# Local attention in steps of two windows: row tiles for the scores, column tiles for the weighted sums

## The chip, the cores and the metric

The kernel runs on one core of one Trainium2 chip. The metric is the device time of one execution in microseconds (us). A core has a matrix engine (TensorE, PE in the profile, with its weight loads as PEld), a vector engine (VectorE, DVE), an activation engine (ScalarE, ACT), a general engine (GpSimd, POOL) and a queue engine that issues transfers (SyncE, SP). Each works through its own list of instructions in order; semaphores join the lists. On chip, data lie in SBUF (128 partitions) and in PSUM, which TensorE writes, in banks of 512 float32 columns per partition.

## The reference, cut to what matters

The program is four blocks of attention and feed-forward on `x` (8 x 256 x 256), with a layer norm before each. The stage that the change touches is the third attention. With 16 heads of 16 elements, windows of 64 rows, and each window attending to itself and to the window before it:

```python
qb = q.reshape(b, h, nb, w, d) * d ** -0.5           # w = 64, d = 16, 4 windows in a batch
kw, vw = look_around(kb), look_around(vb)            # the window before, then this one: 128 keys
sim = jnp.einsum('bhnwd,bhnjd->bhnwj', qb, kw)
sim = jnp.where(mask[None, None], sim, -jnp.finfo(sim.dtype).max)
attn = jax.nn.softmax(sim, axis=-1)
out = jnp.einsum('bhnwj,bhnjd->bhnwd', attn, vw)
...
return x @ W_out.T + b_out
x = x + jnp.tanh(g_xattn[2]) * _L2_xattn_ref(_layernorm(x, axis=-1), ctx_1024, ctx_1024, L2_xattn_W_out, L2_xattn_b_out)
```

## The kernel before

`build` runs nine stages one after the other, with a barrier between them. All but `stage_local_attention` (L1558 to L1912) stay as they are.

**A unit** is one window of one batch: 4 units in a batch, 8 batches, 32 units. The 16 heads are taken as 8 pairs, since a pair's 2 x 64 query rows fill 128 rows. The 256 features lie in two halves (`kt`) of 128 partitions with four pairs in each. GpSimd writes `la_qd` (L1896): for each half, four stationary matrices of 128 x 128, in which only the 32 partitions of the pair hold queries and all others are zero. So each score product runs over all 128 partitions, although 32 of them count.

**One unit on TensorE**, in the names of the trace:
- `front`, L1702 and L1704, twice: a product with the identity puts the mask into a bank of `la_scores` (512 columns), and four products `la_qd` x `la_kT` are added to it. Four banks, so that two units have room.
- `turn`, L1718: eight transposes of `la_e` into two banks `la_turned`.
- `back`, L1730: eight products `la_eT` (stationary, 128 x 128) x `la_vw` (33 columns: the values of a pair of heads and a column of ones for the sum of the weights) into `la_av`.

Each float32 product shows as two pairs of records, weight load and matmul; a transpose as one.

**The other engines.** VectorE takes the maximum of a bank (L1812) and subtracts it while it copies the bank to `la_e` in SBUF (L1817). ScalarE takes the exponent in SBUF (L1778), one instruction for 512 columns, and copies `la_turned` to `la_eT` (L1787). VectorE takes the reciprocal of the 8 sums (L1829) and multiplies (L1833).

**Once a batch.** `prep`: TensorE transposes queries and context (L1685, L1691) through the one bank of `la_misc`, and ScalarE copies them out (L1765, L1770). `final`: TensorE transposes the attention's output (L1739), ScalarE copies it (L1791), TensorE multiplies by `la_woT` (L1746), VectorE adds to `x_res` (L200), and the layer norm follows.

**The order** is written by hand in `batches`: per unit `turn(n)`, `front(n+1)`, `back(n)`, so TensorE has the scores of the next unit to do while the weights of this one are copied. Batches 1 to 6 are a loop over two batches. At the start, GpSimd adds the bias to all 16 tiles of `x_res` (L1914) before its first `la_qd`.

## Time and profile before

| | us |
|---|---|
| median of 3 runs | 2733.89 (2731.76 to 2738.29) |
| the profiled execution | 2743.94 |
| its span | 2742.2 |
| of this, local attention, first instruction to last | 1634.35 to 1877.36 |
| first score product of the stage | 1657.4 |

The profile is one execution, recorded by the hardware. Its span runs from the first to the last instruction; 1.7 us of the execution lie outside. Start times are counted from the span's start. A group of consecutive instructions of one kind stands in one row, with its first start and the time to its last end. Matmuls overlap in the engine, so their starts lie closer together than one takes. The granted clock is a share of TensorE's full speed (2.4 GHz); 0.5 is 1.2 GHz.

### The profile page before, as it was taken

The numbers are of one execution on the slowest core, as the hardware profiler recorded it, in microseconds if no ns is written. First come the engines' busy times: TensorE is split into PE (matmuls) and PEld (weight loads), VectorE is DVE, ScalarE is ACT, GpSimd is POOL, SyncE is SP. The second block draws the span as 40 slices with busy tenths as digits, with TensorE's granted clock in tenths as the row PEclk, the third lists the DMA queues.
The fourth block names the chain that finished last, engine by engine and source line by source line (L and its number), as shares of the span: only waits on it lengthen the run. The fifth ranks groups of instructions, "written<-read, shape, count | busy, mean of one in ns | idle before, by whom it ended". The sixth has DMA issues, their size and how long they took to land. (4 is left out here: it accounts for less than half of the span.)

```text
span 2742.2 us, 39081 instructions
## 1 busy us (share of the span) xinstructions
PE 2031.4 (74%) x12230; PEld 1715.1 (63%) x12265; DVE 1472.1 (54%) x4679; ACT 785.6 (29%) x2012; POOL 512.1 (19%) x670
## 2 busy tenths in 40 slices
PE   4178699999999759999999807885910667777445
PEld 3155477777777759999999807883510655566323
DVE  5789755555555421111111155676577538988856
ACT  2111133333333211111111103442463423333155
POOL 3567610000000040000000064340024320000110
PEclk9589899999999779999999958996965785567569
DMA  2100010000000260032132131211000030111100
GB/s 92 32 1 0 14 73 4 8 8 8 8 8 0 89 236 25 23 117 71 69 117 71 47 97 28 43 21 35 0 0 0 0 109 26 36 28 35 26 21 31
DMA packets 133827, 113.56 MB, mean 41 GB/s; under 512 B 60384, under 2 KB 118760, under 8 KB 133736
## 3 DMA queue, kind: packets, MB, share of 16 engines
q1 hardware_dynamic: 120280, 94.67, 11.3%
q10 hardware_dynamic: 10384, 9.45, 1.0%
q0 software_dynamic: 3072, 8.39, 0.9%
q8 instruction: 38, 0.62, 0.1%
q14 instruction: 53, 0.43, 0.0%
HBM read 78.00 MB, written 24.05 MB: 37 GB/s over the span
## 5 line engine op out<-in xcount | busy, mean ns | idle before, releaser
L1481 DVE TENSOR_TENSOR me_h<-me_sg,me_ps_u 128x512 f32<-128x512 f32 x106 | 72.9, 688 | 346.9 <-PE me_ps_u L1412 346.9
L1412 PE MATMUL me_ps_g<-me_xT,me_w 128*128 128x128 f32 x1696 | 208.5, 276 | 12.9 <-DMA me_w<-in_L_ffn_w_s 12.9
L1412 PEld LDWEIGHTS me_ps_g<-me_xT,me_w 128*128 128x128 f32 x1696 | 203.2, 193 | 16.4 <-DMA me_w<-in_L_ffn_w_s 13.3
L1412 PE MATMUL me_ps_u<-me_xT,me_w 128*128 128x128 f32 x1696 | 207.5, 276 | 0.0
L1421 PE MATMUL me_ps_y<-me_w,me_h 128*128 128x256 f32 x848 | 200.6, 379 | 0.0
L1412 PEld LDWEIGHTS me_ps_u<-me_xT,me_w 128*128 128x128 f32 x1696 | 198.8, 193 | 0.0
L989 ACT ACTIVATE ca_e<-ca_main,ca_neg_max 128x256 f32<-128x256 f32 x256 | 119.1, 470 | 211.0 <-DVE ca_neg_max L1037 211.0
L1421 PEld LDWEIGHTS me_ps_y<-me_w,me_h 128*128 128x128 f32 x848 | 152.9, 190 | 16.4
L1461 ACT ACTIVATE me_sg<-me_ps_g 128x512 f32<-128x512 f32 x106 | 63.3, 597 | 337.6 <-PE me_ps_g L1412 337.6
L902 PE MATMUL ca_main<-ca_kT,ca_qT 128*128 128x256 f32 x512 | 135.9, 394 | 4.4 <-DVE carrier L79 3.6
L925 PE MATMUL ca_av<-ca_v,ca_eT 128*128 128x64 f32 x1024 | 131.1, 272 | 8.5 <-DVE ca_eT L1033 8.5
L1530 POOL DMA_INDIRECT mc_picked<-moe_y_list,moe_slot x32 | 31.3, 978 | 564.4 <-SPq L1507 554.6
L925 PEld LDWEIGHTS ca_av<-ca_v,ca_eT 128*128 128x128 f32 x1024 | 125.3, 193 | 12.6 <-DVE ca_eT L1033 7.8
L2279 PE MATMUL id_ps_h<-ident,id_h 128*128 128x128 f32 x96 | 14.5, 292 | 145.2 <-DVE id_h L2302 145.2
L180 POOL TENSOR_TENSOR ca_ln_rstd<-ca_ln_mean_var,eps 128x1 f32<-128x1 f32 x16 | 3.1, 192 | 560.1 <-DVE ca_ln_mean_var L174 560.1
L2636 PE MATMUL ss_acc<-sc_gm,ss_zT 32*128 32x128 f32 (+2 forms) x368 | 83.5, 379 | 30.3 <-ACT ss_zT L2517 30.3
L2508 ACT ACTIVATE sc_y_all<-ss_v 128x16 f32<-128x16 f32 x256 | 60.4, 236 | 158.3 <-DVE ss_v L2570 156.0
L1486 DVE COPY me_y<-me_ps_y 128x256 f32<-128x256 f32 x53 | 22.5, 424 | 154.7 <-PE me_ps_y L1421 154.7
L2279 PEld LDWEIGHTS id_ps_h<-ident,id_h 128*128 128x128 f32 x96 | 12.3, 151 | 147.6 <-DVE id_h L2302 145.1
L2636 PEld LDWEIGHTS ss_acc<-sc_gm,ss_zT 32*128 32x128 f32 x368 | 67.8, 266 | 54.7 <-ACT ss_zT L2517 54.7
L1026 DVE TENSOR_TENSOR ca_main<-ca_main,ca_mask_add 128x512 f32<-128x512 f32 x128 | 88.8, 694 | 22.6 <-PE ca_main L902 21.3
L902 PEld LDWEIGHTS ca_main<-ca_kT,ca_qT 128*128 128x128 f32 x512 | 90.1, 192 | 16.0 <-DVE carrier L79 6.5
(420 smaller groups left out, 4755.9 us busy)
## 6 DMA issues: line engine op xcount, KB each, us to landing
me_w<-in_L_ffn_w_e SPq DMA_DIRECT2D x24, 1024.0 KB, 8.7
ss_gb<-scan_g_band SPq DMA_DIRECT2D x15, 512.0 KB, 3.9
me_x_tile<-moe_x_list SPq DMA_DIRECT2D x54, 128.0 KB
moe_y_list<-me_y ACTq DMA_DIRECT2D x53, 128.0 KB
moe_x_list<-mr_zeros SPq DMA_DIRECT2D x1, 5248.0 KB, 23.4
la_vw<-in_ctx SPq DMA_DIRECT2D x24, 128.0 KB, 3.4
x_res<-in_x SPq DMA_DIRECT2D x4, 512.0 KB, 8.0
fa_q<-x_norm SPq DMA_DIRECT2D x8, 256.0 KB, 2.4
```

Of the source, the lines that this page charges most:

```text
L902: last = nc.tensor.matmul(ps[:, it * S:(it + 1) * S], qT[:, s // 2, s % 2, it * P:(it + 1) * P], kT[:, s // 2, :], start=True, stop=True)
L925: last = nc.tensor.matmul(ps_av[g % 2][:, o:o + DH], eT[:, h % 2, jt, it * P:(it + 1) * P], v[:, jt, h * DH:(h + 1) * DH], start=(jt == 0) ...
L989: last = nc.scalar.activation(e[:, h % NE, it, :], ps[:, it * S:(it + 1) * S], ACT.Exp, bias=neg_max[:, h % 4, it:it + 1], accum_out=sums[ ...
L1026: nc.vector.tensor_tensor(both, both, mask_add[:, bass.ds(b, 1), :].broadcast_to([P, 2, S]), ALU.add).then_inc(masked, 1)
L1412: last = nc.tensor.matmul(ps[:, j * P:(j + 1) * P], w13[:, buf, w, kt, f:f + P], xT[:, kt, :], start=(kt == 0), stop=(kt == KD - 1))
L1421: last = nc.tensor.matmul(ps_y[:, 0:D], h[:, c, j, :], w2[:, buf, f, :], start=(f == 0), stop=(f == FT - 1))
L1461: nc.scalar.activation(sg[:, c, :], ps_g[c][:, :], ACT.Silu).then_inc(silu_done, 1)
L1481: nc.vector.tensor_tensor(h[:, c, :, :].rearrange("p j n -> p (j n)"), sg[:, c, :], ps_u[c][:, :], ALU.mult).then_inc(h_ready[c], 1)
L1530: nc.gpsimd.indirect_dma_start(out=picked[:, t % BUFS, j, :], out_offset=None, in_=y_list, in_offset=bass.IndirectOffsetOnAxis(ap=slot[:, ...
L2279: last = nc.tensor.transpose(ps_h[c][:, j * P:(j + 1) * P], h[:, par, f * P:(f + 1) * P], core.ident[:, :])
L2508: nc.scalar.activation(y_all[:, :, :, t], by_batch(v[:, :, t]), ACT.Sigmoid).then_inc(y_ready, 1)
L2636: last = nc.tensor.matmul(acc[n % 2][:, h, 0:P].rearrange("p (b t) -> p b t", b=B)[:, :, c0:TB], zT[rows, k, h, :], gm[rows, pair(n, k), : ...
```

## The change

The step is now two windows (`NU` = 2), 16 steps in all, and the loop is written out in full. The stationary operand of a score product is 32 partitions high, one pair of heads, so that four pairs lie in four row tiles of the array, each writing a bank of its own. In the weighted sums the operands are swapped: the values of a pair (32 columns: 16 of one head and 16 zeros, or the reverse, from `la_vz`) are stationary, `la_eT` (64 columns) moves, and four pairs write four column tiles of 32 partitions. The sums of the weights come from the same products with a matrix of ones (`la_ones`), on all 32 partitions, so the reciprocal now has 256 columns. The output comes out transposed, so that L1739 and L1791 go. The maximum is taken negated, the subtraction goes, and ScalarE takes it as the bias of the exponent, straight from PSUM, one instruction for each 128 columns.

```diff
-        def batches(eng, walks, prep, turn, front, back, final, finish):
...
-                    turn(b, par, nb)
-                    if nb < UNITS - 1:
-                        front(b, par, nb + 1)
-                    elif has_next:
-                        front(b + 1, 1 - par, 0)
-                    back(b, par, nb)
...
+        def walk(prep, score, turn, weigh, final, finish):
+
+            prep(0)
+            for n in range(STEPS + 1):
+                b, u = divmod(n, NU)
+                if n >= 1:
+                    for r in range(RT - 1):
+                        turn(n - 1, r)
+                if n < STEPS:
+                    score(n)
+                if n >= 1:
+                    turn(n - 1, RT - 1)
+                if u == 0 and b + 1 < B:
+                    prep(b + 1)
+                if n >= 1:
+                    weigh(n - 1)
+                if u == 1 and b >= 1:
+                    final(b - 1)
+                if u == 0 and b >= 2:
+                    finish(b - 2)
...
+            sp.wait_ge(const, 3)
+            load(0)
...
+            def score(n):
+                b, u = divmod(n, NU)
+                pe.wait_ge(q_ready, n + 1)
...
+                banks = [ws.fill() for _ in range(RT)]
...
+                for ps, _, _ in banks:
+                    nc.tensor.matmul(ps[:, :], ident16[:, :], masks[:, int(u > 0), :, :], start=True, stop=False)
+                for j in range(4):
+                    nb, kt = divmod(j, KD)
+                    lo = W * (NU * u + nb)
+                    for r, (ps, filled, _) in enumerate(banks):
+                        rows = slice(R * r, R * (r + 1))
+                        last = nc.tensor.matmul(ps[:, j * P:(j + 1) * P], qd[rows, n % 2, kt, nb, :],
+                                                kT[rows, b % 2, kt, lo:lo + P], start=False, stop=(j == 3))
...
+            def turn(n, r):
+                ws.when_read(score_bank[n, r])
+                ps, filled, turned_bank[n, r] = wt.fill()
...
+            def weigh(n):
+                b, u = divmod(n, NU)
+                pe.wait_ge(vz_ready, b + 1)
+                for r in range(RT):
+                    wt.when_read(turned_bank[n, r])
                 ps, filled, _ = wa.fill()
...
+                for j in range(4):
+                    nb, kt = divmod(j, KD)
+                    for what in range(2):
+                        o = (4 * what + j) * W
+                        for h in range(2):
+                            for r in range(RT):
+                                lhs = (ones[:, h, :, :] if what else
+                                       vz[:, b % 2, NU * u + nb, RT * kt + r, 2 * h:2 * h + 2, :])
+                                last = nc.tensor.matmul(ps[R * r:R * (r + 1), o:o + W],
+                                                        lhs.rearrange("p a d -> p (a d)"),
+                                                        eT[:, n % 2, r, j, h * W:(h + 1) * W],
+                                                        start=(h == 0), stop=(h == 1))
...
+            def final(b):
+                wa.when_all_read()
...
+            def exponent(n, r):
+                act.wait_ge(max_done, RT * n + r + 1)
+                for j in range(4):
+                    last = nc.scalar.activation(e[:, n % 2, r, j, :], scores.ps[r][:, j * P:(j + 1) * P], ACT.Exp,
+                                                bias=mx[:, n % 2, r, j:j + 1])
+                    if j == 3:
+                        last.then_inc(scores.empty[r], 1)
+
+            def turn(n, r):
+                if r == 0:
+                    exponent(n, 0)
+                if r < RT - 1:
+                    exponent(n, r + 1)
+                ps, empty = wt.drain()
...
+                half = NU * KD * W
+                nc.vector.reciprocal(rsum[:, :], ps[:, half:2 * half]).then_inc(recip, 1)
...
+            nc.gpsimd.memset(vz[:, :, :, :, :, :], 0.0).then_inc(const, 1)
+            nc.gpsimd.memset(vn[0:W, :, 0, :], 0.0).then_inc(const, 1)
...
-            with pool.Fori(0, TILES) as t:
-                nc.gpsimd.tensor_tensor(core.x[:, t, :], core.x[:, t, :], bias[:, :], ALU.add).then_inc(bias_added, 1)
```

TensorE, in the first batch, two units before the change. `la_scores0` to `3` and `la_turned0` and `1` are the banks:

```order
L1718 MATMUL la_turned0<-ident,la_e 128x128 x4
L1718 MATMUL la_turned1<-ident,la_e 128x128 x4
L1702 MATMUL la_scores0<-la_masks,la_ident16 128x512
L1704 MATMUL la_scores0<-la_kT,la_qd 128x128 x4
L1702 MATMUL la_scores1<-la_masks,la_ident16 128x512
L1704 MATMUL la_scores1<-la_kT,la_qd 128x128 x4
L1730 MATMUL la_av0<-la_vw,la_eT 128x33 x8
```

The same place after it, one step of two units: the end of one step's transposes, the scores of the next (the last line comes four times in turn over the banks), and the weighted sums (this pair of lines comes four times):

```order
L1708 MATMUL la_turned0<-ident,la_e 128x128 x4
L1693 MATMUL la_scores0<-la_masks,la_ident16 128x512
L1693 MATMUL la_scores1<-la_masks,la_ident16 128x512
L1693 MATMUL la_scores2<-la_masks,la_ident16 128x512
L1693 MATMUL la_scores3<-la_masks,la_ident16 128x512
L1699 MATMUL la_scores0<-la_kT,la_qd 128x128
L1699 MATMUL la_scores1<-la_kT,la_qd 128x128
L1699 MATMUL la_scores2<-la_kT,la_qd 128x128
L1699 MATMUL la_scores3<-la_kT,la_qd 128x128
...
L1708 MATMUL la_turned1<-ident,la_e 128x128 x4
L1725 MATMUL la_av0<-la_eT,la_vz 32x64 x8
L1725 MATMUL la_av0<-la_eT,la_ones 32x64 x8
```

Before, the scores of one unit use two banks of four. Now a step uses all four, and its first instruction needs all four read.

ScalarE at the same place, before, for two units:

```order
L1778 ACTIVATE la_e<-la_e 128x512 x2
L1787 ACTIVATE la_eT<-la_turned0 128x512
L1787 ACTIVATE la_eT<-la_turned1 128x512
L1778 ACTIVATE la_e<-la_e 128x512 x2
L1787 ACTIVATE la_eT<-la_turned0 128x512
L1787 ACTIVATE la_eT<-la_turned1 128x512
```

And after, for one step:

```order
L1763 ACTIVATE la_e<-la_scores0,la_mx 128x128 x4
L1763 ACTIVATE la_e<-la_scores1,la_mx 128x128 x4
L1776 ACTIVATE la_eT<-la_turned0 128x512
L1763 ACTIVATE la_e<-la_scores2,la_mx 128x128 x4
L1776 ACTIVATE la_eT<-la_turned1 128x512
L1763 ACTIVATE la_e<-la_scores3,la_mx 128x128 x4
L1776 ACTIVATE la_eT<-la_turned0 128x512
L1776 ACTIVATE la_eT<-la_turned1 128x512
```

The exponents of banks 2 and 3 now stand behind copies that wait for TensorE's transposes of the same step.

## Rows read from the trace of the kernel before

**Rows 1.** Busy time by stretch: PE, PEld, DVE, ACT, POOL; granted clock; DMA share, GB/s
```profile
1634.30:1657.40 23.10, 3.32 (x12) 2.15 (x12) 0.35 (x1) 3.08 (x4) 18.03 (x30) 0.50 0.54 102
1657.40:1877.40 220.00, 190.87 (x1470) 178.34 (x1496) 141.55 (x384) 85.86 (x150) 75.83 (x94) 0.97 0.13 27
```

**Rows 2.** Waits of 1657 to 1877.5: waiter, waited for: total us, times, longest
```profile
PE la_turned L1718 <- ACT la_e L1778: 9.7, 18, 1.4
...
PE la_misc L1746 <- ACT la_aoT L1791: 7.2, 8, 0.9
```

**Rows 3.** Timeline, PE, once a batch: start us, us, engine, line, operation, count [idle]
```profile
1725.64 1.97 PE L1746 MATMUL la_misc<-la_woT,la_aoT 128*128 128x256 f32 x8 [0.92 <-ACT la_aoT L1791]
...
1751.71 1.97 PE L1746 MATMUL la_misc<-la_woT,la_aoT 128*128 128x256 f32 x8 [0.92 <-ACT la_aoT L1791]
```

**Rows 4.** Timeline, PE, parts of units at full clock
```profile
1771.43 1.04 PE L1718 MATMUL la_turned<-ident,la_e 128*128 128x128 f32 x8
...
1773.41 0.38 PE L1702 MATMUL la_scores<-la_masks,la_ident 128*128 128x512 bf16 x1
1773.63 1.05 PE L1704 MATMUL la_scores<-la_kT,la_qd 128*128 128x128 f32 x8
1774.52 0.31 PE L1730 MATMUL la_av<-la_vw,la_eT 128*128 128x33 f32 x2
```

**Rows 5.** Groups by line, PE: count | busy us, mean ns | idle before
```profile
L1730 PE MATMUL la_av<-la_vw,la_eT 128*128 128x33 f32 x512 | 60.0, 272 | 0.0
```

**Rows 6.** Timeline, later stages: row tiles (32*128), full array, column tiles (128*32), bfloat16
```profile
2400.21 0.66 PE L2636 MATMUL ss_acc<-sc_gm,ss_zT 32*128 32x128 f32 x4
2400.80 0.60 PE L2627 MATMUL ss_acc<-sc_gm,ss_zT 128*128 128x128 f32 x3
...
2402.32 0.14 PEld L2653 LDWEIGHTS ss_ps_z<-ident,ss_z 128*32 128x32 f32 x2 [0.56 <-DVE ss_z L2606]
...
2660.12 0.62 PE L2970 MATMUL bt_ps_h<-bf_ident,bt_hi 128*128 128x128 bf16 x8 [1.17 <-DVE bt_hi L2933]
```

**Rows 7.** Timeline and groups, ACT: exponents, small activations, the copy of `la_turned`
```profile
821.01 0.47 ACT L989 ACTIVATE ca_e<-ca_main,ca_neg_max 128x256 f32<-128x256 f32 x1 [1.33 <-DVE ca_neg_max L1037]
821.38 0.19 ACT L989 ACTIVATION_READ_ACCUMULATOR ca_e<-ca_main,ca_neg_max 128x1 f32 x1
...
2399.57 0.22 ACT L2508 ACTIVATE sc_y_all<-ss_v 128x16 f32<-128x16 f32 x1
2399.69 0.22 ACT L2512 ACTIVATE ss_az<-ss_v 128x16 f32<-128x16 f32 x1
...
L1221 ACT ACTIVATE mr_ex<-mr_shifted 128x128 f32<-128x128 f32 x1 | 0.3, 309 | 3.6 <-DVE mr_shifted L1248 3.6
...
1781.82 1.09 ACT L1787 ACTIVATE la_eT<-la_turned 128x512 f32<-128x512 f32 x2 [4.18 <-PE la_turned L1718]
```

**Rows 8.** Groups, DVE: reciprocals of 8 and of 96 columns, a product of 256
```profile
L1829 DVE RECIPROCAL la_rsum<-la_av 128x8 f32<-128x8 f32 x32 | 6.6, 206 | 2.5 <-PE la_av L1730 1.6
...
L525 DVE RECIPROCAL f4p_q_rscale<-f4p_q_scale 128x96 f32<-128x96 f32 x2 | 1.5, 752 | 0.1
...
L1047 DVE TENSOR_TENSOR ca_ao<-ca_av,ca_rsums 128x256 f32<-128x256 f32 x64 | 24.2, 419 | 1.1
```

**Rows 9.** Timeline, the stage's start, and GpSimd's largest memset (group)
```profile
L1071 POOL MEMSET ca_qT<- 128x4096 f32 x1 | 3.5, 3512 | 1.3 <-POOLq L93 1.3
...
1643.60 0.35 DVE L1801 TENSOR_SCALAR la_bias<-la_bias,tanh_g 128x256 f32<-128x256 f32 x1 [12.23 <-DMA la_bias<-in_L_xattn_b_out]
...
1648.51 0.60 ACT L1770 ACTIVATE la_kT<-la_misc 128x512 f32<-128x512 f32 x1 [1.21 <-PE la_misc L1691]
1655.18 4.29 POOL L1896 TENSOR_TENSOR la_qd<-la_xT,la_own 128x512 f32<-128x512 f32 x4
```

**Rows 10.** Timeline, the stage's end: the last output product and the last layer norm
```profile
1870.32 3.38 PE L1746 MATMUL la_misc<-la_woT,la_aoT 128*128 128x256 f32 x8 [0.78 <-ACT la_aoT L1791]
...
1876.95 0.41 DVE L194 TENSOR_SCALAR x_norm<-x_res,la_ln_mean_var,la_ln_rstd 128x256 f32<-128x256 f32 x1 [0.44 <-POOL la_ln_rstd L183]
```

More of the change, by code:

```diff
@@ L18 @@
 I32 = mybir.dt.int32
+I16 = mybir.dt.int16
+U16 = mybir.dt.uint16
 U8 = mybir.dt.uint8
@@ L1631, in nothing @@
         def nothing(*_):
             pass
[L1634 to L1640 removed]
         @block.sync
         def _(sp):
[L1644 to L1656 removed]
+            wm = Walk(misc, sp)
@@ L1669, in _ @@
         @block.tensor
         def _(pe):
-            ws, wt, wa, wm = walks(pe)
-            pe.wait_ge(small_in, 32)
-            ps, filled, use = wm.fill()
-            for kt in range(KD):
-                for r in range(2):
-                    last = nc.tensor.transpose(ps[:, (kt * 2 + r) * P:(kt * 2 + r + 1) * P],
-                                               wo[:, r, kt * P:(kt + 1) * P], core.ident[:, :])
-            last.then_inc(filled, 1)
-            def prep(b, par):
-                pe.wait_ge(xs_in[par], 32 * (b // 2 + 1))
+            ws, wt, wa, wm = (Walk(banks, pe) for banks in (scores, turned, av, misc))
@@ L1745, in final @@
                     for kt in range(KD):
-                        last = nc.tensor.matmul(ps[:, h * D:(h + 1) * D], aoT[:, kt, h * P:(h + 1) * P], woT[:, kt, :],
-                                                start=(kt == 0), stop=(kt == KD - 1))
+                        last = nc.tensor.matmul(ps[:, h * D:(h + 1) * D], aoT[:, b % 2, kt, h * P:(h + 1) * P],
+                                                woT[:, kt, :], start=(kt == 0), stop=(kt == KD - 1))
                 last.then_inc(filled, 1)
-            pe.wait_ge(const2, 2)
-            batches(pe, list(zip((ws, wt, wa, wm), PER)), prep, turn, front, back, final, nothing)
+            weights()
+            walk(prep, score, turn, weigh, final, nothing)
         @block.scalar
         def _(act):
-            ws, wt, wa, wm = walks(act)
+            wt, wm = Walk(turned, act), Walk(misc, act)
             nc.scalar.preload_act_table(ACT.Exp)
@@ L1794, in _ @@
-            batches(act, list(zip((ws, wt, wa, wm), PER)), prep, turn, front, nothing, final, nothing)
+            def exponent(n, r):
+                act.wait_ge(max_done, RT * n + r + 1)
+                for j in range(4):
+                    last = nc.scalar.activation(e[:, n % 2, r, j, :], scores.ps[r][:, j * P:(j + 1) * P], ACT.Exp,
+                                                bias=mx[:, n % 2, r, j:j + 1])
+                    if j == 3:
+                        last.then_inc(scores.empty[r], 1)
@@ new lines, in turn @@
+            def turn(n, r):
[4 more added lines that the diff above has]
+                ps, empty = wt.drain()
+                if r == 0 and n >= 2:
+                    act.wait_ge(av.filled[0], n - 1)
+                nc.scalar.activation(eT[:, n % 2, r, :, :].rearrange("p j q -> p (j q)"), ps[:, :], ACT.Copy
+                                     ).then_inc(empty, 1)
+            walk(prep, nothing, turn, nothing, lambda b: wm.skip(1), nothing)
@@ L1796, in _ @@
         @block.vector
         def _(dve):
-            ws, wt, wa, wm = walks(dve)
+            ws, wa, wm = (Walk(banks, dve) for banks in (scores, av, misc))
             wm.skip(1)
@@ L1830, in back @@
                 dve.wait_ge(recip, n + 1)
-                to = W * (nb % 2)
-                for h in range(2):
-                    last = nc.vector.tensor_tensor(
-                        ao[to:to + W, par, nb // 2, :].rearrange("p (g c) -> p g c", g=PAIRS)[:, :, h * DH:(h + 1) * DH],
-                        sums[h * W:(h + 1) * W, :, h * DH:(h + 1) * DH],
-                        rsum[h * W:(h + 1) * W, nb % 2, :].unsqueeze(2).broadcast_to([W, PAIRS, DH]), ALU.mult)
-                last.then_inc(empty, 1)
@@ L1847, in final, with finish @@
                 core.vector_inc(empty)
-            def finish(b, par):
+            def finish(b):
                 for h in range(2):
                     norm.vector_apply(dve, 2 * b + h, h)
-            batches(dve, list(zip((ws, wt, wa, wm), PER)), prep, nothing, front, back, final, finish)
+            walk(lambda b: wm.skip(2), score, nothing, weigh, final, finish)
         @block.gpsimd
@@ L1883, in _, with spread @@
             wm.skip(1)
-            def prep(b, par):
-                xT_use[0] = wm.use()
-                wm.skip(1)
-            def spread(b, par, nb):
-                n = UNITS * b + nb
-                if nb == 0:
-                    wm.when_read(xT_use[0])
-                if not (first_uses(b) and n < 2):
-                    pool.wait_ge(s_ready, 2 * (n - 1))
+            def spread(n):
+                b, u = divmod(n, NU)
+                if n >= 2:
+                    pool.wait_ge(scores.filled[RT - 1], n - 1)
```

302 lines of the change are left out of this document (118 added, 184 removed).

## The prediction

> **What bounds the kernel now.** The nine stages stand one after the other, so only local attention's own time counts. I read it by stretches first [rows 1]: 23.1 us of start with a nearly idle TensorE, then 220.0 us in which TensorE is busy for 190.9, VectorE 141.6, ScalarE 85.9, at a granted clock of 0.97. The waits come next [rows 2]: TensorE waits 9.7 us for exponents and 7.2 us for the copy before the output product, each in pieces of a microsecond. So the list of TensorE itself sets the pace, at 26.07 us a batch, the distance of two output products [rows 3].
>
> Its prices, start to start at full clock [rows 4]: a transpose (1.04 - 0.27) / 7 = 0.110 us; a mask 0.216; a matmul record of the scores (1.05 - 0.28) / 7 = 0.112, two records to a product. The weighted sums have 512 records for 256 products [rows 5]; with the stationary operand already there, 33 columns took 0.31 - 0.28 = 0.03 us [rows 4], otherwise 0.112 like the scores, the load of 128 columns. Two units cost 16 transposes (1.75), 4 masks (0.86), 16 score products (3.58), 16 products of the sums (3.58): 9.8 us. A batch has two of these, 8 transposes of inputs, 4 of the output and 1.8 us of output product, some 22.7 us; the other 3.4 are waits.
>
> **The change, part by part, for a step of two units.**
>
> *Scores.* The same 16 products of 128 columns. A product's two passes share a tile and must follow one another (0.112), but the next product lies in another tile. The list has them in the order tile 0 twice, tile 1 twice, so a second pass can overlap the first pass of the next tile, and no more: 16 x 0.112 = 1.79 us. If row tiles do not overlap, 3.58; if the four tiles ran fully side by side, 4 x 0.224 = 0.90. I take 1.79.
>
> *Weighted sums.* 8 products a unit become 32: 64 a step, of 64 moving and 32 stationary columns. A pass of 64 columns is 2 x 0.03 = 0.06 us by the 33 columns. The load of 32 columns is no limit: two loads take 0.14 us to the end of the second, which alone has some 0.11 [rows 6], so they start 0.03 apart. With the same half overlap 64 x 0.060 = 3.84 us; without it 7.2 to 7.7; with full overlap 1.92. Four instructions in 0.060 us would be 15 ns each; the tightest row has a load and a matmul in (0.62 - 0.22) / 7 = 0.057 [rows 6], so the trace proves only half this rate. I take 3.84, nearest to the price of the pass, and keep both ends.
>
> *Changes of tile shape.* Between a group of row tiles and the full array the starts spread [rows 6]: four matmuls in 0.66 put the last start at 2400.60, the next comes at 2400.80 instead of 0.11 later, and the three after it take 0.60 instead of 0.50. That is 0.19 us, four times a step.
>
> *Exponents.* Four instructions of 128 columns for one of 512. Start to start 256 columns take 0.37 and 16 columns 0.12 [rows 7], so 128 take 0.235; one alone takes 0.309 [rows 7]. A bank is 0.94 us to the next instruction, 1.05 to its end. ScalarE's sum, 16 x 0.235 + 4 x 0.50 for the copies (two in 1.09 [rows 7]) = 5.8 us a step, is far below TensorE's.
>
> But its order counts. The next step's masks need all four banks read, so the exponents of bank 3 stand ahead of them, behind a copy, the exponents of bank 2, another copy, and the transposes that follow the weighted sums. Before, TensorE had spare banks and nothing of this lay on the path. From one step's masks to the next: masks 0.86, change 0.19, scores 1.79, change 0.19; last transposes and their copy 0.44 + 0.17 (a matmul ends 0.28 after its start, the next starts after 0.11) + 0.59 + 0.08 of hand-overs = 1.28; change, weighted sums, change 4.22; first transposes and their copy 0.44 + 0.17 + 0.04 + 0.50 = 1.15; exponents 0.94, copy 0.50, exponents and hand-over 1.09. Sum 12.21 us.
>
> The Trainium skill has a rule against this change: "TensorEngine Tiling (Array Packing)", section "PSUM Bottleneck", says that tiling speeds up TensorE but not the emptying of PSUM, which may become the bottleneck. As a throughput it would give 5.8 us a step for ScalarE, and is no bound here; the rows make the order the bound instead.
>
> *Gone from VectorE and TensorE.* The subtraction lay beside TensorE's work (VectorE is busy for 141.6 of 220 us [rows 1], and TensorE hardly waits for scores' copies), so it is worth nothing alone. The output's transposes and their copy (0.44 + 0.17 + 0.92 idle, about 1.4 us a batch) go from the path.
>
> *Once a batch.* The input's transposes wait for ScalarE to empty one bank: 1.05 us more on the path. The output product now follows the sums directly and waits for a reciprocal of 256 columns: 8 columns take 0.206 and 96 take 0.752 [rows 8], 6.2 ns a column, so 1.75; then a product of 256 columns, 0.42 [rows 8], and hand-overs: 2.4, and 1.8 of output product, 4.2 us. Queued behind this wait stand the first transposes, and behind them the exponents of bank 2. A batch is 2 x 12.21 + 1.05 + 4.2 = 29.7 us, 3.6 above the 26.07 of before.
>
> *Start.* The bias adds (10.94 us of GpSimd ahead of the first `la_qd`, which comes at 1655.18 [rows 9]) are spread over the batches, and `la_qd` is half as wide. But the transfers now wait for three memsets, one of 4096 columns (3.51 us [rows 9]): 4.1 us with the two others. `la_bias` was used at 1643.60, and the copy of `la_kT` ended at 1649.11 [rows 9], 5.5 us later. So the first scores start at 1643.6 + 4.1 + 5.6 = 1653.3 instead of 1657.4: 4.1 us gained. GpSimd's first `la_qd` (half of 4.29 / 4 = 1.07 us each [rows 9]) and its small constants, by my estimate done before the bias lands, hide in this.
>
> *Sum.* From the first masks to the stage's end: first step 8.9 (no sums ahead of it, the first maximum and two banks of exponents exposed), 15 x 12.21 = 183.2, 7 x 1.05 and 7 x 4.2 = 36.8, end 15.0: last transposes 1.3, sums 4.2, reciprocal and product 2.4, output product 3.4 at half clock and from there to the last layer norm 3.7 [rows 10]. Together 243.9 against 220.0, so +23.9, and -4.1 at the start: +19.8 us. The profiled span would go from 2742.2 to 2762; the median, 10 us below this execution, from 2733.9 to 2754.
>
> **The rivals.**
>
> *Full overlap, ends faster.* If a tile's second pass need not hold the next tile, scores 0.90 and sums 1.92: 2.81 us less in each of 16 steps, -45, so -25 us, 2709. It decides at 19.8 / 16 = 1.24 us: scores and sums together below 4.4 us a step instead of 5.63. Against it speaks the order of the list, tile by tile in pairs.
>
> *Partly more overlap, no change.* If scores gained a factor of 3 and sums of 2.4, they would take 1.17 and 3.0 us: 1.46 less a step, -23, in all -4 us, 2730. The Trainium skill, "TensorE: Matmul & The Clock Gate", section "Measured speedup vs the span model", states such factors, 3.07 for four row tiles and 2.38 for three column tiles, for products of 512 columns. No row here has two tiles at once, so none shows it.
>
> *Row tiles do not help.* A stationary operand of 32 partitions still has 128 columns to load. If these loads follow one another, 0.112 each, scores stay at 3.58: +1.79 x 16 = +29, 2782. For it: the sums of before, which pay 0.112 for 33 columns [rows 4]. This is the rival in which half of the change doesn't do what it says.
>
> *No overlap at all.* Sums 7.2 as well: +5.1 x 16 = +82, 2836.
>
> *Clock.* TensorE would be busy for some two thirds of a batch, in gaps of a microsecond, where it now is for nine tenths. In the stage of [rows 10] the last output product, after gaps, ran at half clock (3.38 for 1.97 us). If most did, the passes cost double, over 100 us. Against it: the gaps of before left 0.97 [rows 1].
>
> **How the numbers follow.** About 0.2%, 5.5 us, is what a measurement of this kernel can tell from no change. My forecast, 2754, with its own range of 2740 to 2770 for the unproved prices of exponents and hand-overs: 0.37. Row tiles without gain, 2782: 0.23. No overlap, 2836: 0.13. More overlap, 2730: 0.08. Full overlap or cheaper still, 2709: 0.13. Clock: 0.06. The range from 2716 to 2838 leaves out full overlap and the clock, 0.19. Faster 0.17 (full overlap and some of the row above it), same 0.07, slower 0.76.
>
> **What would show it.** Masks of bank 0 about 12.2 us apart inside a batch, output products 29.7 us apart. Four rows of row-tile matmuls start within 0.9 us, not 0.45 or 0.9 x 2; 64 products of the sums in 3.8 us. TensorE's longest waits in sum are for exponents (`la_e`), some 2.5 us a step, where it was 9.7 us in all. VectorE's reciprocal 1.75 us. First scores at 1653. I am wrong if the sums take under 2.5 or over 5 us, if exponents of 128 columns start much off 0.235 us, or if the clock falls.

## The result, and the profile after

| | kernel before | changed kernel |
|---|---|---|
| median of 10 runs | 2741.58 us | 2756.54 us |
| lowest to highest | 2731.76 to 2745.39 | 2750.46 to 2770.49 |
| profiled execution, span | 2742.2 us | 2753.9 us |
| first masks to last layer norm of local attention | 220.0 us | 235.4 us |

The ratio is 1.0058, 95% interval 1.0036 to 1.0080. The change makes the kernel slower by 15 us. The forecast was 2754 us; the sign and the size hold, but, as the trace shows, not for the reasons given: two terms were far too high and three costs were missing, and they nearly cancelled.

By stretches, the changed kernel (busy time of PE, PEld, DVE, ACT, POOL; granted clock; DMA share, GB/s); the second stretch is one output product. They answer to [rows 1]:

```profile
1651.90:1887.32 235.42, 155.53 (x3000) 115.60 (x3000) 95.74 (x168) 108.05 (x334) 47.70 (x86) 0.85 0.09 27
1754.95:1758.85 3.90, 3.82 (x10) 2.99 (x11) 0.03 (x1) 0.00 (x0) 0.00 (x0) 0.50 0.00 0
```

TensorE has 35 us less work than before (somewhat more than that, since 26 of the 64 mask records of before are missing from its trace) and VectorE 46 less, in 15 us more. The first stretch's clock is 0.85 where it was 0.97. No engine is busy for even 70% of it. This is what a chain across engines looks like in such a table.

Who is waited for, TensorE (total us, times, longest), against [rows 2]:

```profile
PE la_turned L1708 <- ACT la_e L1763: 19.5, 24, 1.7
PE la_misc L1736 <- DVE la_aoT L1800: 18.6, 8, 2.3
PE la_scores L1693 <- ACT la_e L1763: 13.4, 15, 1.0
PE la_av L1725 <- issue: 10.7, 7, 2.0
PE la_av L1725 <- ACT la_eT L1776: 8.8, 10, 0.9
PE la_misc L1679 <- ACT la_xT L1754: 5.9, 8, 0.8
```

One step that prepares inputs and the step with the output product behind it, from the timeline, TensorE and what it waits for (start us, us, engine, line, operation, tiles, count, idle before):

```profile
1734.82 1.02 PE L1693 MATMUL la_scores<-la_masks,la_ident 128*128 128x512 bf16 x4 [0.95 <-ACT la_e L1763]
1735.77 1.17 PE L1699 MATMUL la_scores<-la_kT,la_qd 32*128 32x128 f32 x32
1736.88 0.66 PE L1708 MATMUL la_turned<-ident,la_e 128*128 128x128 f32 x4
...
1739.31 0.43 PE L1725 MATMUL la_av<-la_eT,la_vz 128*32 128x64 f32 x16
...
1741.23 0.66 PE L1708 MATMUL la_turned<-ident,la_e 128*128 128x128 f32 x4
...
1742.42 1.18 ACT L1763 ACTIVATE la_e<-la_scores,la_mx 128x128 f32<-128x128 f32 x4
1743.42 0.67 ACT L1776 ACTIVATE la_eT<-la_turned 128x512 f32<-128x512 f32 x1
...
1743.90 1.22 ACT L1763 ACTIVATE la_e<-la_scores,la_mx 128x128 f32<-128x128 f32 x4
1745.27 1.02 PE L1693 MATMUL la_scores<-la_masks,la_ident 128*128 128x512 bf16 x4 [0.96 <-ACT la_e L1763]
...
1752.42 0.31 PE L1725 MATMUL la_av<-la_eT,la_ones 128*32 128x64 f32 x4 [1.57 <-issue]
...
1752.76 1.76 DVE L1798 RECIPROCAL la_rsum<-la_av 128x256 f32<-128x256 f32 x1 [2.87 <-PE la_av L1725]
...
1755.03 3.78 PE L1736 MATMUL la_misc<-la_woT,la_aoT 128*128 128x256 f32 x8 [2.31 <-DVE la_aoT L1800]
1758.61 1.90 PE L1708 MATMUL la_turned<-ident,la_e 128*128 128x128 f32 x8
...
1763.00 1.14 PE L1693 MATMUL la_scores<-la_masks,la_ident 128*128 128x512 bf16 x4 [0.95 <-ACT la_e L1763]
```

Five things are to be seen.

- **Tiles run four abreast.** All 32 records of the scores fit in 1.17 us, and the next group starts 1.11 after them. All 128 records of the sums start between 1739.31 and 1741.23. A record of 128 columns takes 0.112 us on its tile [rows 4], so 32 on four tiles take 0.90; 128 records of 64 columns at half of that take 1.8. The starts of the single records show how: four come 0.007 us apart, one on each tile, and the next four 0.111 us after them.
- **The chain over ScalarE.** Masks follow masks by 10.45 us here and in two more of the seven steps that prepare inputs; in the other four, parts of which ran at half clock, by 12.0 to 12.9. And the last link is the one forecast: a copy of `la_eT`, the exponents of bank 3, then the masks.
- **A pause without a name.** The sums stop for 1.57 us with 4 records to go, "issue": the profile shows nothing that it waits for. Seven of the 16 steps have one, six of 1.5 to 2.0 us and one of 0.75.
- **The output product waits 2.31 us** for the reciprocal, as forecast, and then runs at half clock (the stretch of 0.50 above, 1.2 GHz), 3.78 us for the 1.97 of [rows 3]. So do the transposes behind it (8 in 1.90 for 1.04 of [rows 4]). All seven output products between steps take 2.6 to 3.8 us; before, two of the seven took 3.6 and the others 1.97.
- Together the step with an output product takes 17.73 us here (1745.27 to 1763.00).

### The profile page after: what moved, and what is told of

Its sections match the earlier page's. It is cut to its first block and busy times, and to the rows that moved or that the text cites. A ratio compares the mean times of both kernels' runs of the same rounds, so it can differ in the third digit from the quotient of the medians.

```text
span 2753.9 us, 41536 instructions
## 1 busy us (share of the span) xinstructions
PE 2001.7 (73%) x13768; PEld 1656.5 (60%) x13769; DVE 1425.5 (52%) x4463; ACT 807.8 (29%) x2196; POOL 476.4 (17%) x655
## 5 line engine op out<-in xcount | busy, mean ns | idle before, releaser
L927 PEld LDWEIGHTS ca_av<-ca_v,ca_eT 128*128 128x128 f32 x1024 | 125.4, 193 | 12.7 <-DVE ca_eT L1035 7.8
```

Of the source, the lines that this page charges most:

```text
L927: last = nc.tensor.matmul(ps_av[g % 2][:, o:o + DH], eT[:, h % 2, jt, it * P:(it + 1) * P], v[:, jt, h * DH:(h + 1) * DH], start=(jt == 0) ...
```

## The experiments

They ran on three chips: e1 to e4 on one, where the kernel before has a median of 2765 us, e5, e6, e8 and e9 on another (2768), e10 and e11 on a third (2767). Each is compared by its ratio to the kernel before on its own chip, and in its trace by the time from the first masks to the last layer norm ("stage", good to some 0.4 us, as some first records are missing). e1 and e2 have 2 runs each, e6, e9 and e11 have 4, the others 10.

Outside the stage the code is the same in all of them, yet there the profiled executions differ: all ahead of it took 18 to 39 us longer than in the first profile of the changed kernel, all behind it 854.6 to 871.9 us. So a difference of a few microseconds between two medians isn't read as the work of an edit.

| run | what | median | ratio, 95% | stage us | clock in it |
|---|---|---|---|---|---|
| e10 | changed kernel | 2777.7 | 1.0041 [1.0017, 1.0064] | 237.3 | 0.83 |
| e1 | scores by tile | 2823.9 | 1.0208 [1.0142, 1.0275] | 279.4 | 0.76 |
| e2 | sums by tile | 2856.4 | 1.0326 [1.0255, 1.0396] | 299.1 | 0.89 |
| e3 | exponents first | 2764.2 | 0.9993 [0.9967, 1.0020] | 216.4 | 0.85 |
| e4 | no late wait | 2750.2 | 0.9958 [0.9933, 0.9984] | 208.4 | 0.90 |
| e5 | wide ones | 2760.0 | 0.9963 [0.9936, 0.9990] | 213.2 | 0.90 |
| e8 | VectorE subtracts | 2757.7 | 0.9957 [0.9936, 0.9978] | 211.2 | 0.88 |
| e6 | e3, e5, product before sums | 2721.3 | 0.9835 [0.9786, 0.9885] | 174.0 | 0.90 |
| e9 | e6, preparation split | 2704.5 | 0.9755 [0.9707, 0.9803] | 158.3 | 0.94 |
| e11 | e9, VectorE subtracts | 2745.0 | 0.9935 [0.9909, 0.9961] | 196.5 | 0.86 |

### The changed kernel once more (e10)

No edit; it is the base for the others, by its ratio, since only e11 ran on the same chip.

> The changed kernel itself, beside the kernel before, on the chip of the experiments, where the kernel before takes 2765 to 2768 us instead of 2742. The experiments so far point to one number: each of their medians, less the change that its own trace shows between the first masks and the last layer norm of local attention, gives 2777 to 2792, mostly 2780 to 2783. Theory 'the change costs the same share here': 1.0058 x 2767 = 2783, ratio 1.003 to 1.008. Rival 'the experiments were compared across chips, and the changed kernel is as fast as the kernel before here': ratio under 1.002; then none of the gains of the smaller edits may be read from the ratios.

Ratio 1.0041, inside the first theory's bounds, and its interval overlaps that of the first measurement. The expectation speaks of one chip of the experiments. There were three, but the kernel before has medians within 3 us of each other on them. The smaller edits' gains may be read against it.

### Do the tiles overlap because of the list's order? (e1, e2)

The two parts of the change that use tiles, each with its list turned round:

```
-                for j in range(4):
-                    for r, (ps, filled, _) in enumerate(banks):
+                for r, (ps, filled, _) in enumerate(banks):
+                    for j in range(4):
```

> The same 16 score products a step, listed tile by tile (four of tile 0, then four of tile 1) instead of column block by column block. Theory 'order': the tiles overlap only because neighbours in the list lie in different tiles. Then the 32 records of a step take some 16 x 0.224 = 3.58 us less what little still overlaps where the tile changes, instead of 0.95, and the program gets 16 x 2.6 = 42 us longer: about 2798 against 2756. Rival 'size': a product with only 32 rows is cheap wherever it stands (its operand loads in a quarter of the time). Then the group stays at about 0.95 us and the time at 2756.

```
-                for j in range(4):
...
-                            for r in range(RT):
+                for r in range(RT):
+                    for j in range(4):
```

> The same 64 products of the weighted sums, tile by tile (16 of column tile 0, then 16 of tile 1). Theory 'order': the 128 records take 64 x 0.11 to 0.12 = 7 to 7.7 us instead of 1.99, so 16 x 5 to 5.7 = 80 to 90 us more: about 2840. Pauses of TensorE between these records for want of instructions (1.6 to 2.2 us in seven steps of the changed kernel) should then go, since the list is consumed at a quarter of the rate, and give 10 to 13 us back: about 2830. Rival 'size': a product of 32 stationary columns and 64 moving ones costs 0.03 us wherever it stands; the group stays at 2 us, the time at 2756 and the pauses stay.

The scores of one step in e1, at full clock (timeline, TensorE):

```profile
1835.38 2.82 PE L1699 MATMUL la_scores<-la_kT,la_qd 32*128 32x128 f32 x32
```

and the first and last records of a step's sums in e2, with the output product behind:

```profile
1848.39 0.38 PE L1725 MATMUL la_av<-la_eT,la_vz 128*32 128x64 f32 x4 [0.88 <-ACT la_eT L1776]
1848.61 0.39 PE L1725 MATMUL la_av<-la_eT,la_ones 128*32 128x64 f32 x4
...
1854.73 0.39 PE L1725 MATMUL la_av<-la_eT,la_ones 128*32 128x64 f32 x4
1857.42 1.99 PE L1736 MATMUL la_misc<-la_woT,la_aoT 128*128 128x256 f32 x8 [2.31 <-DVE la_aoT L1800]
```

The order theory holds. The same 64 products of the sums take 6.7 us instead of 2.0, and four records come in the 0.22 us in which sixteen did. The scores take 2.82 us at full clock, less than 3.58, because the end of one tile still overlaps the start of the next (the first record of the second tile starts after 0.55 us, when three of the first tile's eight are still to start, so the engine doesn't keep the list's order there): 1.65 more a step, 26 us. In seven of the 16 steps they ran at half clock (5.13), 2.3 us more each. Together that is the 42 us that the stage lost, but only roughly, since other parts moved too: the pauses fell from 8.4 us in e10 to 3.4.

In e2 the 64 products cost 4.7 us more in each step, 76 in all, less 8.4 of pauses; the stage lost 62, the median 79. The pauses in the sums are gone, and the output product is at full clock in six of the seven batches, after the same wait of 2.31 us. So what is paid for in both is the columns of a tile, 0.112 us for 128, whether they belong to one product or to another.

### Is ScalarE's order the length of a step? (e3)

```
                 if r == 0:
-                    exponent(n, 0)
-                if r < RT - 1:
-                    exponent(n, r + 1)
+                    for k in range(RT):
+                        exponent(n, k)
```

> ScalarE does the exponents of all four banks of a step first and the four copies behind them; nothing else is moved. Theory 'order of ScalarE': the next step's masks wait for the exponents of banks 2 and 3, each behind a copy, and that is the length of a step. With all exponents first the bank is read 0.7 + 4.3 = 5.0 us after the scores' end, and then the third transposes, which need the first copy (0.6 more) and take 0.44, are last: a step of 1.95 + 5.6 + 0.44 = 8.0 us inside a batch instead of 9.5 to 10.45. 15 steps by 1.5 to 2.4: 22 to 36 us less, 2720 to 2734, if no pause for want of instructions or clock takes its place. Rival 'supply or clock': the pauses between TensorE's instructions and the half-clock stretches, not ScalarE, set the pace; then it stays within 5 us of 2756. The waits of TensorE at the transposes for the first bank's exponents should get longer by one theory (ScalarE is late with the copy) and stay by the other.

The stage falls by 21 us, the median by 13.5: below the expected 22 to 36. The wait of the masks for exponents is gone, but at full clock the step that prepares inputs is no shorter (1754.79 to 1765.20 between masks, 10.41 us for 10.45). ScalarE's part of that step:

```profile
1757.33 0.60 ACT L1775 ACTIVATE la_eT<-la_turned 128x512 f32<-128x512 f32 x1 [1.96 <-PE la_turned L1708]
1757.82 0.60 ACT L1754 ACTIVATE la_xT<-la_misc 128x512 f32<-128x512 f32 x1
...
1759.17 0.60 ACT L1757 ACTIVATE la_kT<-la_misc 128x512 f32<-128x512 f32 x1 [0.74 <-PE la_misc L1679]
...
1759.66 4.23 ACT L1763 ACTIVATE la_e<-la_scores,la_mx 128x128 f32<-128x128 f32 x16
...
1763.65 1.21 ACT L1775 ACTIVATE la_eT<-la_turned 128x512 f32<-128x512 f32 x2
1764.52 0.63 PE L1708 MATMUL la_turned<-ident,la_e 128*128 128x128 f32 x4 [1.99 <-ACT la_eT L1775]
```

The first bank's maxima are there at 1757.4, but the inputs' copies stand ahead, the second waiting 0.74 us for TensorE, which waits for the first; the exponents begin 2.2 us late. My expectation left these copies out. Of the 21 us some 9 are gained in the six steps with an output product between their masks, where the exponents now run beside its wait, 2.5 in the one late step without inputs (11.07 us in e10, 8.57 here) and 1.8 in the second step. Another 4.6 lie in steps with inputs, five of which had been longer than 10.5 us in e10 by parts at half clock.

### The wait of the output product (e4)

```
             def final(b):
-                wa.when_all_read()
+                if b == B - 1:
+                    wa.when_all_read()
```

The output product of batch b - 1 is listed behind the sums of batch b's first step, and `when_all_read` waits for those as well. It needs only the sums of one step earlier, and the single bank `la_av` was not filled again before these had been read.

> The output product of a batch no longer waits until the sums just issued (which belong to the next batch) are read by VectorE; the data that it needs was read one step earlier, and the fill of the single bank of sums has waited for that already. Only the last output product keeps the wait. Theory 'final's wait on the path': seven waits of 2.3 us go, 16 us; and if these waits are what drops the clock to half (output products of 2.6 to 3.8 us for 1.97, and transposes behind them), 1 to 2.5 us more each time, 7 to 17 us: 2724 to 2740. Rival 'ScalarE takes it': the exponents behind this place are then what TensorE waits for instead, and only the clock's part comes back or nothing: 2745 to 2756.

The median falls by 27.5 us, the stage by 29. One step of e4 (timeline, TensorE):

```profile
1844.03 0.33 PE L1725 MATMUL la_av<-la_eT,la_ones 128*32 128x64 f32 x9 [1.40 <-issue]
1844.29 1.99 PE L1737 MATMUL la_misc<-la_woT,la_aoT 128*128 128x256 f32 x8
1846.12 1.04 PE L1708 MATMUL la_turned<-ident,la_e 128*128 128x128 f32 x8
1848.44 0.66 PE L1708 MATMUL la_turned<-ident,la_e 128*128 128x128 f32 x4 [1.29 <-ACT la_e L1764]
```

Product and transposes are back at full clock (1.99 and 1.04 us), as in five of the seven batches. Seven waits of 2.3 us are 16 us; the other 12 or 13 go with the clock, 0.90 in the stage for 0.83. The pauses "issue" stay, eight of them here.

### The pauses: supply of instructions? (e5)

Sums of exponents as 8 products of 256 columns a step instead of 32 of 64:

```
+                for h in range(2):
+                    for r in range(RT):
+                        nc.tensor.matmul(ps[R * r:R * (r + 1), half:2 * half],
+                                         ones[:, h, :, :].rearrange("p a d -> p (a d)"),
+                                         eT[:, n % 2, r, :, h * W:(h + 1) * W], start=(h == 0), stop=(h == 1))
```

> The sums of the exponents (products with the ones) are made by 8 products of 256 moving columns a step instead of 32 of 64: the same columns and results, 48 records of 128 fewer... that is, 80 records a step where there were 128. By the 14 ns a record of the changed kernel the 64 records with values take 0.9 us and 16 of 256 columns on four tiles 4 x 0.107 = 0.43, together 1.33 instead of 1.8: 16 x 0.5 = 8 us less. Theory 'instruction supply': TensorE's pauses inside the sums (1.6 to 2.2 us in seven steps) come because the straight list is consumed faster than it is brought; with 48 fewer records of TensorE a step they go or shrink to below 1 us each, another 7 to 12 us. Together 15 to 20 us below the changed kernel, which by the ratio 1.0058 is expected 1.0058 times the kernel before: ratio 0.9985 to 1.0005. Rival 'the pause belongs to the place' (something else stops TensorE there, say a wait that the profile does not name): seven pauses of the same length stay and only 8 us go: ratio 1.003.

Timeline, TensorE, the sums of one step and the output product behind them:

```profile
1758.13 1.07 PE L1720 MATMUL la_av<-la_eT,la_ones 128*32 128x256 f32 x16 [0.88 <-ACT la_eT L1779]
1758.99 1.10 PE L1728 MATMUL la_av<-la_eT,la_vz 128*32 128x64 f32 x64
1762.42 1.99 PE L1739 MATMUL la_misc<-la_woT,la_aoT 128*128 128x256 f32 x8 [2.33 <-DVE la_aoT L1803]
```

No pause is left in any of the 16 steps (8.4 us in e10). But the sums themselves are hardly shorter: 16 wide records take 0.86 us, where the 64 narrow ones had 0.89. My 14 ns a record was an accident of 64 columns on four tiles; the price is the columns. So of 24 us in the stage 8.4 are the pauses, and the rest goes with the clock, 0.90 for 0.83: TensorE's busy time falls from 160.0 to 139.3 us for the same columns. That fewer instructions, or a slower consumption of them (e2), each end the pauses supports a supply of instructions that falls behind. The page of the changed kernel's profile fits (a queue for instructions: packets, MB, share); the same queue has 38 packets before, where the steps run in a loop, and 50 in e5:

```profile
q8 instruction: 56, 0.92, 0.1%
```

It would have to be the supply of a burst and not the mean rate: e9, below, takes up at least 14.0 matmul records a microsecond in its stage (2212 in 158.4 us), the changed kernel 12.7, and e9 has no pause. What exactly runs empty no run shows, and no run has the new steps in a loop.

### The maximum by ScalarE's bias, undone (e8)

```
+                    nc.vector.tensor_tensor(e[:, n % 2, r, :, :], ps[:, :].rearrange("p (j s) -> p j s", s=P),
+                                            mx[:, n % 2, r, :].unsqueeze(2).broadcast_to([P, 4, P]), ALU.add
+                                            ).then_inc(s_ready, 1)
...
-                for j in range(4):
-                    last = nc.scalar.activation(e[:, n % 2, r, j, :], scores.ps[r][:, j * P:(j + 1) * P], ACT.Exp,
-                                                bias=mx[:, n % 2, r, j:j + 1])
+                nc.scalar.activation(flat, flat, ACT.Exp).then_inc(e_ready, 1)
```

> The part 'max by ScalarE's bias' alone is undone: VectorE subtracts the maximum into SBUF and frees the bank, ScalarE takes one exponential of 512 columns a bank instead of four of 128. Theory 'exponents on the path': two groups of four exponents (1.2 us each) stand between the scores and the next masks; the next masks no longer wait for any exponent, only the third transposes do, and each group costs 0.5 to 0.6: 1.2 us less in each of 15 steps, 18 us. But VectorE has four subtractions (about 0.65 each) more before it comes to the reciprocal, so the sums are read some 2.5 us later and the output product's wait of 2.3 us becomes 4 to 5: 7 x 2 = 14 us more. In sum within 8 us of the changed kernel: ratio 1.003 to 1.008. Rival 'VectorE becomes the bound': its list per step is then 2.5 + 2.7 + 2.2 us plus the layer norm, and the step follows it: more than 15 us slower than the changed kernel, ratio over 1.011. Rival 'bias form was the whole loss': ratio under 1.000.

Ratio 0.9957: the rival "bias form was the whole loss" names this value. The waits of e8 (TensorE):

```profile
PE la_misc L1736 <- DVE la_aoT L1803: 25.0, 8, 4.6
PE la_turned L1708 <- ACT la_e L1763: 12.4, 18, 1.2
```

A step inside a batch takes 8.77 us instead of 10.45, a gain of 1.7 where I expected 1.2, and the output product's wait grows by 6.5 us in all where I expected 14. So in the order of the changed kernel the bias form costs 20 to 26 us, more than the whole loss of the change. It was not the only such part: e4 and e5 each remove as much.

### Three edits together, and the inputs' copies taken apart (e6, e9)

e6 joins e3 and e5 and moves the output product ahead of the sums:

```
+                if u == 1 and b >= 1:
+                    final(b - 1)
                 if n >= 1:
                     weigh(n - 1)
-                if u == 1 and b >= 1:
-                    final(b - 1)
```

> Three edits together: all exponents of a step before the copies (ScalarE), the output product before the sums of the next batch instead of behind them (so it needs nothing that is not long read), and the ones as wide products. Theory 'order': the step with inputs stays at 10.4 us, because ScalarE has the two copies of the inputs ahead of the exponents there; the step with the output product becomes 1.95 + 0.6 + 4.3 + 0.6 + 0.44 = 8 us instead of 13 to 15, so a batch 18.5 instead of 27 to 29. From the first masks to the end of the last output product 228 becomes about 170, the ratio to the kernel before 1.0058 - 58/2760 = 0.985. Rival 'supply': at this pace the list of TensorE cannot be brought fast enough, pauses of 2 us appear in every step (16 x 2 = 32 us) and the ratio is 0.996. Rival 'clock': TensorE idles for longer stretches during the exponents, falls to half clock, and the ratio stays above 0.993.

Ratio 0.9835, stage down by 63 us: "order" is right and both rivals are out. The steps are longer than I expected, though: 11.05 us with inputs and 9.3 to 9.4 with an output product, for 10.4 and 8. In e9 the first input's transposes also stand before a step's third transposes, and its copy behind theirs on ScalarE:

```
+                if more:
+                    prep_part(2, b + 1)
+                if n >= 1:
+                    turn(n - 1, RT - 2)
+                if more:
+                    prep_part(1, b + 1)
                 if n < STEPS:
                     score(n)
```

(`prep_part(2, ...)` acts on TensorE, `prep_part(1, ...)` on ScalarE.)

> The kernel with the three edits, and the preparation of the next batch taken apart: the first input's transposes stand before the third transposes of a step and its copy behind their copy on ScalarE, the second input's stay where they are. Theory 'order of ScalarE': in the step with inputs the exponents then wait for one copy less and the wait of TensorE for the emptied bank goes: the step falls from 10.4 to 8.5 to 9 us, 7 x 1.6 = 11 us less than the kernel with the three edits, ratio lower by 0.004. Rival: the input copies are only moved on ScalarE, which is busy throughout, so the ratio stays within 0.001.

Ratio 0.9755. The step with the inputs falls from 11.06 us in e6 to 9.06, 2 us where I expected 1.6 (the ratio 0.008 where I expected 0.004), and the whole is 73 us faster than the changed kernel by the medians (79 in the stage), 2.4% faster than the kernel before. A step with an output product in e9, from the timeline:

```profile
1758.51 0.81 PE L1707 MATMUL la_scores<-la_masks,la_ident 128*128 128x512 bf16 x3
1759.25 1.17 PE L1713 MATMUL la_scores<-la_kT,la_qd 32*128 32x128 f32 x32
...
1760.84 1.89 PE L1753 MATMUL la_misc<-la_woT,la_aoT 128*128 128x256 f32 x8
...
1761.54 4.23 ACT L1782 ACTIVATE la_e<-la_scores,la_mx 128x128 f32<-128x128 f32 x16
...
1762.66 1.07 PE L1734 MATMUL la_av<-la_eT,la_ones 128*32 128x256 f32 x16
...
1766.39 0.63 PE L1722 MATMUL la_turned<-ident,la_e 128*128 128x128 f32 x4 [0.31 <-ACT la_eT L1794]
1767.07 0.81 PE L1707 MATMUL la_scores<-la_masks,la_ident 128*128 128x512 bf16 x3
```

8.57 us, and 10.1 in two of the six such steps, where the changed kernel needs 14.8 to 17.7. The output product waits for nothing and fills TensorE while ScalarE copies and takes exponents.

### The bias form once more, in the right order (e11)

e9 with the subtraction of e8.

> The kernel with the three edits and the split preparation, and VectorE's subtraction instead of ScalarE's bias. In the changed kernel's order the subtraction saved 24 us between the first masks and the last norm. Theory 'the bias form cost time only by its place': with all exponents ahead of the copies, the last of them ends 4.9 us after the scores with the bias form, and 0.5 + 8 x 0.73 + 0.62 = 7.0 us with the subtraction (eight VectorE instructions start to start at 0.73, then one exponent), so the subtraction now costs up to 1.5 us a step, part of it hidden: 10 to 25 us slower than that kernel, ratio 0.979 to 0.985. Rival 'the bias form is worse anywhere' (ScalarE 4.2 us for its exponents where 2.4 would do): ratio under 0.973.

Ratio 0.9935, 40 us slower than e9 where I expected 10 to 25, so the direction is that of the first theory and the size is not. VectorE now stands in the chain (timeline):

```profile
1724.84 0.69 DVE L1809 TENSOR_TENSOR la_e<-la_scores,la_mx 128x512 f32<-128x512 f32 x1
...
1725.65 0.88 DVE L202 SCALAR_TENSOR_TENSOR x_res<-la_misc,tanh_g,x_res 128x256 f32<-128x256 f32 x2
...
1727.53 1.75 DVE L1819 RECIPROCAL la_rsum<-la_av 128x256 f32<-128x256 f32 x1
1727.77 0.63 PE L1693 MATMUL la_misc<-ident,la_xs 128*128 128x128 f32 x4 [2.82 <-DVE carrier L81]
```

The residual comes behind eight instructions of 0.73, and with it the one bank `la_misc`, for which TensorE's input transposes wait 2.82 us; half clock follows (masks 1.5 to 1.9 us). So, measured with the clock that came with it, the bias form costs 20 to 26 us in one order and saves 40 in the other.

## Why the prediction was right, and where it was not

The number held: 2754 forecast, 2756.5 measured, slower. A part of that is the base: three runs of the kernel before had a median of 2733.9, ten have 2741.6, so the change cost 15 us and not the 20 forecast; the profiled span is 2753.9 for a forecast of 2762, 11.7 us more where 19.8 was forecast. By its own signs of being wrong the mechanism failed in two of three places: the sums took under 2.5 us, and the clock fell. Output products came 25.5 to 29.6 us apart, 27.7 in the mean, for 29.7. Its parts:

- **Scores, 1.79 us, and sums, 3.84 us: wrong.** Measured 0.92 and about 1.8, four abreast, the ends of my bounds. The step that failed is "the next product lies in another tile ... so a second pass can overlap the first pass of the next tile, and no more". A tile's passes do follow one another by 0.111 us, but the three other tiles start theirs meanwhile, 0.007 us apart, so a second pass holds back none of them. This was the premise of the rival with 0.13: scores and sums together took 2.7 us, under its 4.4. Its 2709 failed by the costs below. The Trainium skill, "TensorE: Matmul & The Clock Gate", section "Measured speedup vs the span model", also states a model by which a pack of tiles lasts one matmul and some 4 ns for each further tile. The trace nearly agrees: one record of the scores lasts 0.270 us and a pack of four 0.290, which is 7 ns for each further tile. The factor of 3.07 from the same section, which stood in a rival, is too low here (3.58 by 0.92 us is 3.9); its 2.38 is for three column tiles, and these are four (6.7 by 2.0 us is 3.4).
- **Changes of tile shape, 0.19 us: nearly right.** The last scores' record starts at 1736.68, its pass takes 0.11, and the transposes start at 1736.88. With the second start of each group, which also comes late, the four changes of a step cost 0.12 to 0.20, together 0.6 us for 0.76.
- **The order on ScalarE: right**, and the main loss. With the tiles as measured (2.9 us less) the forecast step with inputs, 13.26, becomes 10.35; measured 10.45 where it ran at full clock. ScalarE is busy for only 108 of 235.4 us, so it is indeed its order that counts. Exponents start every 0.250 us, not 0.235, and a last one ends at 1.14 to 1.23, not 1.05. e3, e6 and e9 remove this chain piece by piece. The forecast of "some 2.5 us a step" of waits for `la_e` was 2.1 (19.5 and 13.4 over 16 steps).
- **Reciprocal 1.75, wait 2.4: right**, 1.76 and 2.31. I took the wait as given; e4 shows that the data did not need it.
- **Output product 1.8 us: wrong**, 2.6 to 3.8 in all seven batches, together 9.9 us more than at 1.97. The clock rival of 0.06 came half true: with the gaps came half clock (0.85 in the stage, 0.97 before), but by the sum below it cost at most some 27 us, not over 100.
- **The pauses "issue": missing**, 10.7 us. Nothing in the kernel before shows them; its records come 0.112 us apart, those of the new scores 0.028 and of the new sums 0.014 in the mean. That its steps ran in a loop and the new ones are written out stood in the diff, and I gave it no price.
- **Start, 4.1 us gained: too low.** The sum counts from the first masks, 1657.4 before and forecast at 1653.3; they came at 1651.9, 5.5 us earlier. The three memsets put off the use of `la_bias` by 2.7 us (1646.30), not by 4.1; from there to the masks it was 5.6, as forecast. That the first scores, behind masks of 1.87 us at half clock, start at 1653.75 is chance.

The sum: 243.9 us forecast from first masks to the end, less 16 x 2.9 = 46 for the tiles, is 197.5; measured 235.4. Of the 38 between them, 10.7 are pauses and 9.9 the output products; the remaining 17 lie where records are at half clock (the first three steps, with masks at 1.87 us for 1.02, the transposes behind the output products, the end), and I can't divide them further. So terms 46 us too high met costs of 38 that were left out. The right number is luck to that extent. The mechanism "TensorE's saving is lost to a chain over ScalarE and VectorE" is shown by e3 and e4, which change the order alone and gain 21 and 29 us in the stage, and by e6 and e9, where the same tiles, with the order changed and fewer instructions, run 1.65% and 2.4% faster than the kernel before. How much of these gains is the shorter chain itself and how much the clock that rose with it they don't divide.

## What to carry to other kernels

When an engine's work becomes less, look next at the order on the engines that hand it its buffers: copies that stand ahead of what frees a bank, and waits for "everything read" where one earlier read would do. Tiles of the array need neighbours in the list that lie in different tiles; the two passes of a float32 product don't disturb that. A part such as the maximum by ScalarE's bias has no price of its own: it cost 20 to 26 us in one order and saved 40 in another.

## What the hardware showed that I had not expected

- Four tiles give nearly a factor of four for float32: 32 row-tile records start within 0.92 us, 3.6 in sequence by [rows 4]; 64 products of the sums take 2.0 us against 6.7 tile by tile. Records of the next tile start before the last three of this one (e1), so the starts don't keep the list's order.
- A record costs its columns, 0.87 ns each on a tile: 16 records of 256 columns on four tiles take 0.86 us, 64 of 64 columns 0.89.
- TensorE stops, mostly for 1.3 to 2.0 us, inside a list of short matmuls, with nothing to wait for that the profile shows, where 128 of them stand in a row and start about 14 ns apart; not with 80 in a row (e5, e6, e9, e11), nor at some 51 ns a record (e2).
- The wait of 2.3 us ahead of the output product was followed by half clock in all seven batches of the changed kernel, but in only one of seven in e2, where TensorE worked for 6.7 us ahead of the same wait, in four of seven in e1 and five of seven in e5. Taking it away (e4) gave back about 4 us a time. In the kernel before, with a wait of 0.92, it was two of seven.
